# A graph layer on one core: ScalarE copies the last 16 items, and GpSimd makes every low part of h

## The chip, the core and the metric

The kernel runs on one core of a Trainium2 chip. The core has five engines that run their own instruction streams and meet at semaphores: TensorE (PE in the profile), VectorE (DVE), ScalarE (ACT), GpSimd (POOL), and SyncE (SP), which here only issues transfers. The metric is the device time of one execution in microseconds, lower is better.

## What is computed

```python
def _L0_gnn_ref(user_feat, item_feat, adj, W_item, b_item, W_user, b_user):
    h = item_feat @ W_item.T + b_item        # 10000 x 128
    b = user_feat @ W_user.T + b_user        # 10000 x 128
    return jax.nn.relu(adj @ h + b)          # adj is 10000 x 10000
x = _layernorm(x + _L0_gnn_ref(x, L0_gnn_item_feat, adj, ...), axis=-1)
```

Everything is float32. The product `adj @ h` is nearly all of the work: 400 MB of `adj` are read once and multiplied.

## The kernel before

**Products in parts.** TensorE takes operands of type fp32r, float32 rounded to fewer bits. So each operand is split: a high part (the rounded copy, made by ScalarE) and a low part (the value minus its high part, made by a subtraction). `adj @ h` is then three products: high x high and high x low (both read `adj_hi`; the second uses `h_lo`), and low x high (`adj_lo` with `h_hi`).

**Groups and tiles.** The users are cut into 20 groups, 19 of 512 and one of 272. Within a group TensorE adds up over 78 full chunks of 128 items, in 20 tiles of four chunks; a full tile is 12 matmuls of 128x512. The last tile (t = 19, `LAST`) has two full chunks, one chunk for `x @ W_user.T` (its weights are `h_hi` and `h_lo` at place `USER`), and one packed matmul, `h_pack` with `tail_pack`, for the last 16 items and the bias.

**Pipeline of `adj`.** SP loads a tile of 1 MB into one of five slots (`ADJ_RING`) once `lo_made` says that VectorE has finished with what was in it. ScalarE makes `adj_hi` (`split_hi`, L519), VectorE makes `adj_lo` (`split_lo`, L714, a `tensor_tensor` with two inputs in SBUF), both in four slots (`PART_RING`): the high part of a tile waits until TensorE is through with the tile four before it. TensorE waits for `hi_made`, does eight matmuls, waits for `lo_made`, does four.

**Start.** Before group 0, TensorE projects the items (`project_items`, L440) into four PSUM buffers, VectorE adds the bias (`add_item_bias`, L679) into `h_full`, ScalarE makes `h_hi` (`split_h`, L536), and GpSimd (t = 0 to 8, L640) or VectorE (t = 9 to 19, `split_h_lo`, L697) makes `h_lo`. The last projection (L444) reads `items_tail`, three copies of the last 16 items, which VectorE puts in place (`copy_items_tail`, L690). Tile 0 of `adj` is split in two halves between these steps (L526 on ScalarE, L722 on VectorE). After its last `h_lo`, GpSimd also makes one row group of `h_pack` (L645) and the low part of `w_user` (L649). In group 0 TensorE waits for `h_lo` of tile t before tile t, and before tile 19 also for `h_pack` and for `w_lo_made`, the signal of L649.

**Order of the work.** Each engine's order is that in which the code calls it; small tables of tile numbers (`HIGH_HALF_AFTER`, `LOW_HALF_AFTER`, `LATE_BLOCK_AFTER`, `POOL_LOWS`, `LOW_BLOCKS_FROM`) say after which tile a step stands. From group 1 on, the engines also do the layer norm of the group before; there GpSimd has two instructions in each group (L657 and L661).

Of the kernel before, what the change touches and what calls it, by code (L numbers as in the profile page):

```python
# [26 lines left out]
P = 128  # L27
# [46 lines left out]
LATE_BLOCK_AFTER = {3: 16, 5: 17, 7: 18, 9: 19}  # L74
TAIL_AFTER_ADD = 16
POOL_LOWS = 9
LOW_BLOCKS_FROM = 4

# [121 lines left out]
def gnn_kernel(nc, adj_t, adj_tail, x_t, adj_narrow, tail_narrow, x_narrow, item_t, w_item_bias, w_user_t, b_user, out, out_last):  # L200
    with ExitStack() as ctx:
# [74 lines left out]
        h_lo_made = sem("h_lo_made")  # L276
        h_lo_made_dve = sem("h_lo_made_dve")
        h_pack_made = sem("h_pack_made")
# [146 lines left out]
        def _(pe):  # L425
# [58 lines left out]
            for t in range(TILES):  # L484
                if t == LAST:
                    pe.wait_ge(w_lo_made, 1)
                    pe.wait_ge(h_pack_made, 1)
                if t < POOL_LOWS:
                    pe.wait_ge(h_lo_made, t + 1)
                else:  # L490
                    pe.wait_ge(h_lo_made_dve, t + 1 - POOL_LOWS)
                tile_product(0, t, 0)
# [10 lines left out]
        def _(act):  # L503
# [24 lines left out]
            def split_h(t):  # L528
# [6 lines left out]
                k = t * PER_TILE  # L535
                nc.scalar.copy(h_hi[:, k:k + n, :], h_full[:, k:k + n, :]).then_inc(h_hi_made, 1)  # L536

            def gather(n):
# [67 lines left out]
            for t in range(EARLY_BLOCKS):  # L606
                split_h(t)
                if t in HIGH_HALF_AFTER:
                    split_hi_half(HIGH_HALF_AFTER.index(t))
            for t in range(1, TILES):  # L610
                if t == LAST:
# [16 lines left out]
        def _(pool):  # L628
# [6 lines left out]
            nc.gpsimd.memset(items_tail[:, :], 0.0).then_inc(items_tail_zeroed, 1)  # L635
            for t in range(POOL_LOWS):
                n = full_chunks(t)
# [4 lines left out]
            again = slice(PACK_HI_AGAIN, PACK_HI_AGAIN + PACKED_ROWS)  # L642
            pool.wait_ge(h_lo_made, POOL_LOWS)
            pool.wait_ge(h_hi_made, TILES)
            nc.gpsimd.tensor_tensor(h_pack[again, :], h_tail[again, :],  # L645
# [26 lines left out]
        def _(dve):  # L672
            def add_item_bias(t):
# [3 lines left out]
                if t == LAST:  # L677
# [3 lines left out]
                                        ALU.add).then_inc(h_full_made, 1)  # L681

            def copy_items_tail():

                dve.wait_ge(items_tail_zeroed, 1)
                dve.wait_ge(item_landed[item_load(LAST)], 16)
                cols = (FULL - LAST * PER_TILE) * P
                landed = item_tiles(LAST, cols + TAIL)[:, cols:cols + TAIL]
                packs = items_tail[:, 0:len(PACKS) * PACK_LO].rearrange("p (n c) -> p n c", c=PACK_LO)[:, :, 0:TAIL]
                nc.vector.tensor_copy(packs, landed[:, None, :].to_broadcast([P, len(PACKS), TAIL])).then_inc(  # L690
                    items_tail_made, 1)

            def split_h_lo(t):
                n = full_chunks(t)
                k = t * PER_TILE
                dve.wait_ge(h_hi_made, t + 1)
                nc.vector.tensor_tensor(h_lo[:, k:k + n, :], h_full[:, k:k + n, :],  # L697
                                        h_hi[:, k:k + n, :].bitcast(F32), ALU.subtract).then_inc(h_lo_made_dve, 1)

# [130 lines left out]
            for t in range(TILES):  # L830
                add_item_bias(t)
                if t == TAIL_AFTER_ADD:
                    copy_items_tail()
                if t in LOW_HALF_AFTER:
                    split_lo_half(LOW_HALF_AFTER.index(t))
            for t in range(1, TILES):
                split_lo(0, t)
                if t >= LOW_BLOCKS_FROM and POOL_LOWS + t - LOW_BLOCKS_FROM < TILES:
                    split_h_lo(POOL_LOWS + t - LOW_BLOCKS_FROM)
            group(1, 1)  # L840
# [52 lines left out]
```

## Time and profile before

| | |
|---|---|
| three runs | 1086.23, 1086.39, 1086.84 us (median 1086.39) |
| the profiled execution | 1085.97 us, of which the span of the trace is 1084.1 us |
| TensorE busy | 1078.3 us, 99% of the span |
| VectorE, ScalarE, GpSimd busy | 962.1, 835.7 and 115.8 us |
| granted TensorE clock | 0.999 |
| transfers | 417.14 MB, 385 GB/s over the span |

In the timeline each row has the start from the beginning of the span, the time that it took, engine, line, operation, what is written and read with shapes, how many instructions are merged in the row, and, in brackets, how long the engine stood idle before it and what ended that. An engine starts its next instruction some 0.1 us before the recorded end of the one before when nothing holds it back, so a merged row is shorter than its instructions added up. A wait on a transfer is shown as DMA. PEld is the loading of weights into TensorE, which runs beside the matmuls.

### The profile page before, as it was taken

The page shows a single profiled execution, that of the slowest core. Times are in us where ns is not written, and L with a number is a line of the kernel's source. Part 1 is how long each engine was busy: PE and PEld are TensorE (multiplying, and loading weights), DVE is VectorE, ACT ScalarE, POOL GpSimd, SP SyncE. Part 2 cuts the span into 40 slices and gives each one's busy share as a digit, 9 for nine tenths or more (in the row PEclk, how much of TensorE's full clock was granted, in tenths as well). Part 3 has the DMA queues.
Part 4 walks back from the last instruction along what each step waited for, and adds up shares of the span by engine and source line. Part 5 has one row for each costly group of instructions (what it writes and reads, how often), then busy time and mean ns, then how long its engine had stood idle before and what let it go on. Part 6 is the DMA issues. An engine that isn't in the chain of part 4 may idle for free.

```text
span 1084.1 us, 14876 instructions
## 1 busy us (share of the span) xinstructions
PE 1078.3 (99%) x4935; PEld 901.3 (83%) x4935; DVE 962.1 (89%) x614; ACT 835.7 (77%) x801; POOL 115.8 (11%) x56
## 2 busy tenths in 40 slices
PE   9999999999999999999999999999999999999998
PEld 9888888888888888888888888888888888888888
DVE  6998898989898989898989898989898989898987
ACT  5877787878787878787878787878787878787775
POOL 4270000000000000000000000000000000000001
PEclk9999999999999999999999999999999999999999
DMA  9999999999999999999999999999999999999993
GB/s 356 419 382 420 352 422 356 422 370 423 366 422 360 422 376 423 364 422 355 423 359 422 362 423 358 423 359 422 364 422 358 421 358 422 359 422 359 419 350 154
DMA packets 66408, 417.14 MB, mean 385 GB/s; under 512 B 8194, under 2 KB 9284, under 8 KB 20052
## 3 DMA queue, kind: packets, MB, share of 16 engines
q1 hardware_dynamic: 66100, 416.68, 96.5%
q8 instruction: 13, 0.21, 0.1%
q10 hardware_dynamic: 288, 0.20, 0.1%
q14 instruction: 7, 0.06, 0.0%
HBM read 411.72 MB, written 5.12 MB: 385 GB/s over the span
## 4 chain that ended last, share of the span: by engine, by line
PE 99%; DVE 1%; DMA 0%; issue 0%; SPq 0%; DVEq 0%
PE acc L458 32%; PE acc L457 32%; PE acc L464 32%; PE h_ps L440 1%; PE acc L461 0%; DMA items<-item_t 0%; DVE adj_lo L722 0%; DVE h_full L679 0%; DVE stats L781 0%; PE h_ps L444 0%; SPq L335 0%; DVE items L804 0%; SPq L399 0%; DVE items L797 0%; PE z_ps L472 0%
## 5 line engine op out<-in xcount | busy, mean ns | idle before, releaser
L714 DVE TENSOR_TENSOR adj_lo<-adj,adj_hi 128x2048 fp32r<-128x2048 f32 (+2 forms) x391 | 864.8, 2230 | 106.2 <-ACT adj_hi L519 105.8
L519 ACT CAST adj_hi<-adj 128x2048 fp32r<-128x2048 f32 (+2 forms) x391 | 724.3, 1864 | 144.1 <-DMA adj<-adj_t 95.4
L457 PE MATMUL acc<-adj_hi,h_hi 128*128 128x512 f32 (+1 forms) x1580 | 604.3, 384 | 0.0
L458 PE MATMUL acc<-adj_hi,h_lo 128*128 128x512 f32 (+1 forms) x1580 | 604.3, 384 | 0.0
L464 PE MATMUL acc<-adj_lo,h_hi 128*128 128x512 f32 (+1 forms) x1580 | 417.2, 384 | 0.0
L458 PEld LDWEIGHTS acc<-adj_hi,h_lo 128*128 128x128 f32 x1580 | 296.7, 188 | 58.4
L457 PEld LDWEIGHTS acc<-adj_hi,h_hi 128*128 128x128 f32 x1580 | 296.6, 188 | 58.4
L464 PEld LDWEIGHTS acc<-adj_lo,h_hi 128*128 128x128 f32 x1580 | 292.6, 188 | 58.4
L657 POOL TENSOR_TENSOR items<-items,minus_mean 128x512 f32<-128x512 f32 x19 | 39.3, 2068 | 586.4 <-ACT minus_mean L552 586.4
L661 POOL TENSOR_TENSOR items<-items,rstd_all 128x512 f32<-128x512 f32 x19 | 37.6, 1981 | 339.9 <-ACT rstd_all L573 339.9
L544 ACT COPY gathered<-part 32x16 f32<-32x16 f32 x152 | 30.8, 203 | 22.1 <-DVE part L752 12.3
L565 ACT ACTIVATE std<-total,eps 32x16 f32<-32x16 f32 x19 | 5.8, 308 | 44.4 <-DVE total L769 44.4
L645 POOL TENSOR_TENSOR h_pack<-h_tail,h_pack 17x128 fp32r<-17x128 f32 x1 | 26.1, 26053 | 27.8 <-ACT h_hi L536 27.8
L573 ACT COPY rstd_all<-rstd 32x16 f32<-32x16 f32 x76 | 15.4, 203 | 14.4 <-DVE rstd L776 13.7
L552 ACT ACTIVATE minus_mean<-total 32x16 f32<-32x16 f32 x76 | 16.2, 214 | 6.4 <-DVE total L763 5.5
L679 DVE TENSOR_TENSOR h_full<-h_ps,w_bias 128x512 f32<-128x512 f32 (+1 forms) x20 | 13.3, 674 | 7.4 <-PE h_ps L440 7.4
L536 ACT CAST h_hi<-h_full 128x512 fp32r<-128x512 f32 (+1 forms) x20 | 12.0, 606 | 8.0 <-DVE h_full L679 8.0
L709 DVE TENSOR_TENSOR tail_pack<-tail_in,tail_pack 16x512 fp32r<-16x512 f32 (+1 forms) x20 | 13.5, 676 | 0.6
L711 DVE TENSOR_TENSOR adj_lo<-xg,adj_hi 128x512 fp32r<-128x512 f32 (+1 forms) x20 | 13.8, 688 | 0.3
L746 DVE STREAM_TRANSPOSE items<-items 128x512 f32<-128x512 f32 x19 | 13.4, 704 | 0.0
L730 DVE SCALAR_TENSOR_TENSOR items<-acc,xg 128x512 f32<-128x512 f32 x19 | 13.0, 684 | 0.0
L752 DVE TENSOR_REDUCE part<-items 128x16 f32<-128x512 f32 x19 | 12.8, 675 | 0.0
(51 smaller groups left out, 153.8 us busy)
## 6 DMA issues: line engine op xcount, KB each, us to landing
adj<-adj_t SPq DMA_DIRECT2D x360, 1024.0 KB, 7.7
adj<-adj_t SPq DMA_DIRECT2D x21, 512.0 KB, 5.3
adj<-adj_narrow SPq DMA_DIRECT2D x11, 952.0 KB, 7.5
xg<-x_t SPq DMA_DIRECT2D x19, 256.0 KB, 8.0
out<-items SPq DMA_DIRECT2D x19, 256.0 KB, 2.3
tail_in<-adj_tail SPq DMA_DIRECT2D x57, 32.0 KB, 4.6
adj<-item_t SPq DMA_DIRECT2D x2, 512.0 KB, 6.7
adj<-item_t SPq DMA_DIRECT2D x1, 1024.0 KB, 8.7
```

The lines of the kernel that those rows point to most:

```text
L457: nc.tensor.matmul(into, h_hi[:, k, :], high[:, c, :], start=(k == 0), stop=False)
L458: nc.tensor.matmul(into, h_lo[:, k, :], high[:, c, :], start=False, stop=False)
L464: mm = nc.tensor.matmul(into, h_hi[:, k, :], low[:, c, :], start=False, stop=(k == FULL - 1))
L519: nc.scalar.copy(into[:, places[0]:places[-1] + 1, :], source[:, places[0]:places[-1] + 1, :]).then_inc(hi_made, 1)
L544: ins = nc.scalar.copy(gathered[:, q, :], part[q * SQ:q * SQ + SQ, :])
L552: ins = nc.scalar.mul(minus_mean[q * SQ:q * SQ + SQ, :], total[:, :], -1.0 / HID)
L573: ins = nc.scalar.copy(rstd_all[q * SQ:q * SQ + SQ, :], rstd_32[:, :])
L645: nc.gpsimd.tensor_tensor(h_pack[again, :], h_tail[again, :], h_pack[again, :].bitcast(F32), ALU.subtract).then_inc(h_pack_made, 1)
L657: nc.gpsimd.tensor_tensor(centred, z_b, minus_mean[:, :, None].to_broadcast([P, BANDS, SQ]), ALU.add).then_inc(centred_made, 1)
L661: nc.gpsimd.tensor_tensor(z_b, centred, rstd_all[:, :, None].to_broadcast([P, BANDS, SQ]), ALU.mult).then_inc(out_ready, 1)
L711: nc.vector.tensor_tensor(into[:, AT_USER, :], xg[:, 0:u], high[:, AT_USER, :].bitcast(F32), ALU.subtract).then_inc(lo_made, 1)
L714: nc.vector.tensor_tensor(into[:, places[0]:places[-1] + 1, :], source[:, places[0]:places[-1] + 1, :], high[:, places[0]:places[-1] + 1, ...
```

## The change

The copy of the last 16 items goes from VectorE (behind the bias of t = 16) to ScalarE (behind the second half of tile 0's high part). The low parts of h of t = 9 to 19 go from VectorE (one behind each of the subtractions of tiles 4 to 14) to GpSimd, behind its first nine. GpSimd's instructions for `h_pack` and `w_user` stay behind all of its low parts.

```diff
-TAIL_AFTER_ADD = 16
-POOL_LOWS = 9
-LOW_BLOCKS_FROM = 4
...
-                if t < POOL_LOWS:
-                    pe.wait_ge(h_lo_made, t + 1)
-                else:
-                    pe.wait_ge(h_lo_made_dve, t + 1 - POOL_LOWS)
+                pe.wait_ge(h_lo_made, t + 1)
                 tile_product(0, t, 0)
...
+            def copy_items_tail():
+
+                act.wait_ge(items_tail_zeroed, 1)
+                act.wait_ge(item_landed[item_load(LAST)], 16)
+                cols = (FULL - LAST * PER_TILE) * P
+                landed = item_tiles(LAST, cols + TAIL)[:, cols:cols + TAIL]
+                packs = items_tail[:, 0:len(PACKS) * PACK_LO].rearrange("p (n c) -> p n c", c=PACK_LO)[:, :, 0:TAIL]
+                nc.scalar.copy(packs, landed[:, None, :].to_broadcast([P, len(PACKS), TAIL])).then_inc(
+                    items_tail_made, 1)
...
                 if t in HIGH_HALF_AFTER:
                     split_hi_half(HIGH_HALF_AFTER.index(t))
+                if t == HIGH_HALF_AFTER[-1]:
+                    copy_items_tail()
...
-            for t in range(POOL_LOWS):
+            for t in range(TILES):
                 n = full_chunks(t)
                 k = t * PER_TILE
                 pool.wait_ge(h_hi_made, t + 1)
                 nc.gpsimd.tensor_tensor(h_lo[:, k:k + n, :], h_full[:, k:k + n, :],
                                         h_hi[:, k:k + n, :].bitcast(F32), ALU.subtract).then_inc(h_lo_made, 1)
             again = slice(PACK_HI_AGAIN, PACK_HI_AGAIN + PACKED_ROWS)
-            pool.wait_ge(h_lo_made, POOL_LOWS)
-            pool.wait_ge(h_hi_made, TILES)
+            pool.wait_ge(h_lo_made, TILES)
...
             for t in range(TILES):
                 add_item_bias(t)
-                if t == TAIL_AFTER_ADD:
-                    copy_items_tail()
                 if t in LOW_HALF_AFTER:
                     split_lo_half(LOW_HALF_AFTER.index(t))
             for t in range(1, TILES):
                 split_lo(0, t)
-                if t >= LOW_BLOCKS_FROM and POOL_LOWS + t - LOW_BLOCKS_FROM < TILES:
-                    split_h_lo(POOL_LOWS + t - LOW_BLOCKS_FROM)
```

The removed functions `copy_items_tail` and `split_h_lo` of VectorE held the same operations with VectorE's own semaphore for `h_lo`.

VectorE's order around the end of the start and the first tiles of group 0, before the change (from the second half of tile 0 on; the pair of L697 and L714 then repeats up to tile 15):

```order
L722 TENSOR_TENSOR adj_lo<-adj,adj_hi 128x1024
L679 TENSOR_TENSOR h_full<-h_ps,w_bias 128x512
L690 COPY items_tail<-items 128x3x16
L679 TENSOR_TENSOR h_full<-h_ps,w_bias 128x512 x2
L678 TENSOR_TENSOR h_tail<-h_ps,w_bias 128x128
L679 TENSOR_TENSOR h_full<-h_ps,w_bias 128x256
L714 TENSOR_TENSOR adj_lo<-adj,adj_hi 128x2048 x4
L697 TENSOR_TENSOR h_lo<-h_full,h_hi 128x512
```

The same place in the changed kernel, up to tile 19 (there L709 is the half of tile 0, L683 the bias, L701 the low part of an `adj` tile, L696 and L698 the packed tail and the user chunk of tile 19):

```order
L709 TENSOR_TENSOR adj_lo<-adj,adj_hi 128x1024
L683 TENSOR_TENSOR h_full<-h_ps,w_bias 128x512 x3
L682 TENSOR_TENSOR h_tail<-h_ps,w_bias 128x128
L683 TENSOR_TENSOR h_full<-h_ps,w_bias 128x256
L701 TENSOR_TENSOR adj_lo<-adj,adj_hi 128x2048 x18
L696 TENSOR_TENSOR tail_pack<-tail_in,tail_pack 16x512
L698 TENSOR_TENSOR adj_lo<-xg,adj_hi 128x512
```

The copy and the eleven `h_lo` are gone, and the subtractions of tiles 1 to 18 stand one behind the other.

GpSimd's order before the change, from its last step of preparation to the first instruction of the layer norm:

```order
L635 MEMSET items_tail 128x128
L640 TENSOR_TENSOR h_lo<-h_full,h_hi 128x512 x9
L645 TENSOR_TENSOR h_pack<-h_tail,h_pack 17x128
L649 TENSOR_TENSOR h_lo<-w_user,h_hi 128x128
L657 TENSOR_TENSOR items<-items,minus_mean 128x512
```

And in the changed kernel:

```order
L640 MEMSET items_tail 128x128
L645 TENSOR_TENSOR h_lo<-h_full,h_hi 128x512 x19
L645 TENSOR_TENSOR h_lo<-h_full,h_hi 128x256
L649 TENSOR_TENSOR h_pack<-h_tail,h_pack 17x128
L653 TENSOR_TENSOR h_lo<-w_user,h_hi 128x128
L661 TENSOR_TENSOR items<-items,minus_mean 128x512
```

Eleven more low parts stand ahead of `h_pack` and of `w_user`'s low part.

## Rows read from the trace of the kernel before

**Rows 1.** The page: the chain that ended last, shares of the span by engine.

```profile
PE 99%; DVE 1%; DMA 0%; issue 0%; SPq 0%; DVEq 0%
```

**Rows 2.** Timeline, TensorE: last projections, tiles 0 and 1, start of tile 19.

```profile
18.16 5.08 PE L440 MATMUL h_ps<-w_bias,items 128*128 128x128 f32 x44
23.37 0.30 PEld L444 LDWEIGHTS h_ps<-w_bias,items_tail 128*128 128x128 f32 x2 [0.33 <-DVE items_tail L690]
...
23.62 0.47 PE L457 MATMUL acc<-adj_hi,h_hi 128*128 128x512 f32 x1
...
26.46 0.39 PE L457 MATMUL acc<-adj_hi,h_hi 128*128 128x512 f32 x1
...
28.28 1.07 PE L464 MATMUL acc<-adj_lo,h_hi 128*128 128x512 f32 x4
...
75.42 0.39 PE L457 MATMUL acc<-adj_hi,h_hi 128*128 128x512 f32 x1
```

**Rows 3.** Timeline, VectorE, 19 to 82 us.

```profile
19.06 1.22 DVE L722 TENSOR_TENSOR adj_lo<-adj,adj_hi 128x1024 fp32r<-128x1024 f32 x1
...
23.14 0.18 DVE L690 COPY items_tail<-items 128x48 f32<-128x48 f32 x1
...
25.48 2.29 DVE L714 TENSOR_TENSOR adj_lo<-adj,adj_hi 128x2048 fp32r<-128x2048 f32 x1 [0.45 <-ACT adj_hi L519]
...
35.22 0.68 DVE L697 TENSOR_TENSOR h_lo<-h_full,h_hi 128x512 fp32r<-128x512 f32 x1
...
63.59 8.89 DVE L714 TENSOR_TENSOR adj_lo<-adj,adj_hi 128x2048 fp32r<-128x2048 f32 x4
72.51 0.83 DVE L709 TENSOR_TENSOR tail_pack<-tail_in,tail_pack 16x512 fp32r<-16x512 f32 x1
73.36 0.86 DVE L711 TENSOR_TENSOR adj_lo<-xg,adj_hi 128x512 fp32r<-128x512 f32 x1
74.14 7.92 DVE L714 TENSOR_TENSOR adj_lo<-adj,adj_hi 128x1024 fp32r<-128x1024 f32 x4
```

**Rows 4.** Timeline, ScalarE, 19 to 71 us.

```profile
19.98 1.04 ACT L526 CAST adj_hi<-adj 128x1024 fp32r<-128x1024 f32 x1
...
23.54 1.92 ACT L519 CAST adj_hi<-adj 128x2048 fp32r<-128x2048 f32 x1 [1.40 <-DMA adj<-adj_t]
26.03 1.92 ACT L519 CAST adj_hi<-adj 128x2048 fp32r<-128x2048 f32 x1 [0.58 <-DMA adj<-adj_t]
...
62.19 1.92 ACT L519 CAST adj_hi<-adj 128x2048 fp32r<-128x2048 f32 x1 [0.54 <-DMA adj<-adj_t]
...
69.90 0.29 ACT L613 CAST h_hi<-w_user 128x128 fp32r<-128x128 f32 x1
```

**Rows 5.** Timeline, GpSimd, 7 to 74 us.

```profile
7.36 1.27 POOL L640 TENSOR_TENSOR h_lo<-h_full,h_hi 128x512 fp32r<-128x512 f32 x1 [5.72 <-ACT h_hi L536]
9.06 9.92 POOL L640 TENSOR_TENSOR h_lo<-h_full,h_hi 128x512 fp32r<-128x512 f32 x8 [0.43 <-ACT h_hi L536]
46.75 26.05 POOL L645 TENSOR_TENSOR h_pack<-h_tail,h_pack 17x128 fp32r<-17x128 f32 x1 [27.77 <-ACT h_hi L536]
72.88 0.79 POOL L649 TENSOR_TENSOR h_lo<-w_user,h_hi 128x128 fp32r<-128x128 f32 x1
```

**Rows 6.** Timeline, VectorE and GpSimd in a later group.

```profile
209.41 2.29 DVE L714 TENSOR_TENSOR adj_lo<-adj,adj_hi 128x2048 fp32r<-128x2048 f32 x1 [0.19 <-ACT adj_hi L519]
...
210.30 2.31 POOL L657 TENSOR_TENSOR items<-items,minus_mean 128x512 f32<-128x512 f32 x1 [31.11 <-ACT minus_mean L552]
...
212.14 2.62 DVE L714 TENSOR_TENSOR adj_lo<-adj,adj_hi 128x2048 fp32r<-128x2048 f32 x1 [0.44 <-ACT adj_hi L519]
```

**Rows 7.** Timeline, GpSimd near the end, VectorE idle.

```profile
1075.82 1.05 POOL L661 TENSOR_TENSOR items<-items,rstd_all 128x512 f32<-128x512 f32 x1 [9.30 <-ACT rstd_all L573]
```

**Rows 8.** VectorE's groups of instructions by form, usual duration of L709 and L711 (us busy, mean ns).

```profile
L711 DVE TENSOR_TENSOR adj_lo<-xg,adj_hi 128x512 fp32r<-128x512 f32 x19 | 13.3, 701 | 0.3
L709 DVE TENSOR_TENSOR tail_pack<-tail_in,tail_pack 16x512 fp32r<-16x512 f32 x19 | 13.1, 689 | 0.6
```

More of the change, by code:

```diff
@@ L276, in gnn_kernel @@
         h_lo_made = sem("h_lo_made")
-        h_lo_made_dve = sem("h_lo_made_dve")
         h_pack_made = sem("h_pack_made")
@@ L681, in add_item_bias @@
                                         ALU.add).then_inc(h_full_made, 1)
[L683 to L698, printed above, removed]
             def split_lo(g, t):
```

## The prediction

> **What bounds the kernel now.** I read the chain that ended last first: 99% of it is TensorE, and transfers and issue are nothing [rows 1]. Then the timeline of TensorE: from the first product of tile 0 at 23.62 it does not stop; tile 1 begins at 26.46 and tile 19 at 75.42, 18 tiles in 48.96 us, 2.72 each, which is twelve matmuls of 0.227 with no gap [rows 2]. So the kernel is some 24 us of start and then a full TensorE. An edit can gain only in the start, and it costs whatever makes TensorE stand still even once, as nothing later makes that good. The change touches no matmul. What it touches are three things that TensorE waits for: `items_tail_made` before the last projection, `h_lo` of each tile, and the signal of L649 (low part of `w_user`) before tile 19.
>
> In the start, TensorE's last projection waited 0.33 us for VectorE's copy [rows 2, 3]. In group 0, VectorE is ahead of need by little: the low part of tile 1 ended at 25.48 + 2.29 = 27.77 and was read at 28.28 [rows 2, 3]. GpSimd's last two signals come at 46.75 + 26.05 = 72.80 and 72.88 + 0.79 = 73.67, the second 1.75 us before tile 19 [rows 2, 5]. That 1.75 us is the cover that this prediction is about.
>
> **How the two engines share.** The strangest row is GpSimd's L645: 17x128 elements, 26.05 us. It was released at 46.75 and ended at 72.80, and in that whole time VectorE went from one two-input subtraction into the next without a gap; the first place where one ended before the next began is 63.59 + 8.89 = 72.48 to 72.51, and 0.32 us later L645 was done [rows 3, 5]. So a waiting GpSimd instruction doesn't get its turn between two VectorE instructions that follow closely; it needs an opening, and 0.03 us is one. The next one agrees: L649 was released at 72.88 and ended 0.33 us after the opening at 73.34 [rows 3, 5].
>
> VectorE pays for it. L709 took 0.83 in place of 0.69 and L711 0.86 in place of 0.70 [rows 3, 8]: 0.15 us each for a GpSimd instruction 128 wide, with the opening 0.18. For 512 wide there is a later group: VectorE's L714 ended at 211.70, GpSimd's L657 at 212.61, 0.91 later, and the next L714, issued at 212.14, took 2.62 in place of 2.29; so it was held until 211.70 + 0.77 [rows 6]. Alone, this kind of instruction takes 1.05, so 0.14 lie before the hold [rows 7]. But `h_lo` isn't that kind: it writes fp32r, and takes 1.27, or 1.24 in a row [rows 5]. With the same 0.14 before and 0.14 behind, it holds VectorE 1.27 - 0.28 = 0.99 us. The low bound is the 0.77 of L657. I take 0.98, because the 0.33 of L649, which is also fp32r, fits a line through 1.13 at 512 (2.1 ns per column and nearly no fixed part).
>
> The Trainium skill, "SBUF — State Buffer", section "Who interferes with whom", says that a VectorE instruction with two SBUF inputs and a GpSimd instruction that reads SBUF exclude each other, the later one waiting until the first finishes. The exclusion agrees with L645 and L709; "until the first finishes" does not, as L645 sat through more than ten of them. By the page the sum below would be that of the second rival.
>
> **The change part by part.** (1) The copy on ScalarE. It stands behind L526, which ends at 21.02 [rows 4]. Its load is the one that tiles 18 and 19 of the items came from, and TensorE ran through these without a gap up to 23.24 (44 matmul halves in 5.08) [rows 2], so it had landed by some 22. ScalarE's next real deadline is the high part of tile 1, whose transfer lets it start only at 23.54 [rows 4]. So 0.2 us there cost nothing, and TensorE's last projection no longer waits: 23.37 becomes about 23.25, -0.1 us. Were the cover gone, the copy would cost its 0.2.
>
> (2) VectorE loses eleven L697 of 0.68, 0.60 each in a row [rows 3], 6.6 us. It wasn't what TensorE waited for, so this gains nothing; but it makes openings: L714 takes 2.20 in a row (8.89 for four, the last 2.29) [rows 3], and the high parts come 2.49 apart [rows 4]. That is 0.29 us per tile.
>
> (3) GpSimd's nine low parts end at 9.06 + 9.92 = 18.98, and the tenth is ready to go then, against VectorE's first half of tile 0, issued at 19.06 [rows 3, 5]. Whoever is first, each half is late by at most one hold. The bias steps between them read only one SBUF input and GpSimd's eight in a row kept 1.24 beside them [rows 5], so GpSimd uses these: about four passes, t = 9 to 12, by 26. TensorE needs the half tiles only in tile 0, some 4 us later, and tile 1's low part at 28.2; it now ends at 27.8 to 28.9. SP loads tile 5 behind the second half and tile 6 behind tile 1's low part; ScalarE was a tile ahead of TensorE all along, which covers a microsecond there. Cost 0 to 0.7; I take 0.1, which cancels (1).
>
> (4) Then seven passes are left (t = 13 to 19; the last is 256 wide, hold 0.46), and each needs an opening. A pass makes VectorE late by 0.98, and at 0.29 per tile it has caught up, and the next opening is there, after three tiles. Counted in one: for the low part of t = 19 to go in ahead of tile 18, VectorE must have had room for the six before it. The high part of tile 1 ends at 25.46; that of tile 16 begins at 62.19 [rows 4], two more at 2.49 put the end of tile 18's at 69.1. Less 17 subtractions at 2.20 (37.4), the room is 69.1 - 25.5 - 37.4 = 6.2 us. Needed: 6 x 0.98 = 5.9, and some 0.5 of the pass that still runs when tile 1 is due, 6.4. So by 0.2 us it isn't there. Then the last low part goes into the opening ahead of L709 (about 71.5, needed at 75.4), `h_pack` into the one ahead of L711 (72.6), and both of the openings that served L645 and L649 before are taken. With a hold of 0.77 the need is 4.6 + 0.5 = 5.1, and it all fits; the point from which it decides is (6.2 - 0.5) / 6 = 0.95 us.
>
> (5) L649 is late next. Behind L711 come the 1024-wide part of tile 19 and three L714 of group 1, and before the change these ran in one row from 74.14 to 82.06 [rows 3]. TensorE stands at 75.4 before all of tile 19, as it waits there first. The high part of group 1's fourth tile needs tile 19 done, so VectorE runs dry after the third L714 at the latest, and that opening can't be missed. VectorE is about a microsecond earlier than before, as it has no L697: 81.2, plus 0.33, is 81.5. Stall 81.5 - 75.4 = 6.1 us. If it catches up one L714 earlier, 79.0, the stall is 3.9; by the row before as it stands, 7.0. I take 5.9 as I hold the latest opening to be the likelier. Once TensorE goes on, its buffers are full, and nothing is added.
>
> Sum: -0.1 + 0.1 + 5.9, against the profiled execution's own 1085.97 (span 1084.10 and 1.87 around it), 1091.9; that execution is 0.4 below the median of 1086.39. I say **1092.0**.
>
> **The rivals.** *It all fits* (not slower; 0.39). GpSimd's hold is nearer 0.77, or one more pass goes by before tile 1; the margin is 0.2 us in 6.4, so this is nearly as likely. L649 then waits only for its input (69.9 before [rows 4]) and takes the opening ahead of L709, 1.7 us or more before need. Time: 1086.4, up to 1087.1 with what (3) may cost.
>
> *Turn by turn* (0.04). If a waiting GpSimd instruction comes in after each VectorE one, the seven passes follow each other from tile 1 on, at 2.20 + 0.98 = 3.18 per tile against TensorE's 2.72: 7 x 0.46 = 3.2, less 0.5 of slack, 2.7 lost: 1089.1. L645 speaks against it.
>
> *GpSimd keeps the way* (0.08). Its instructions in a row (1.24 apart) may leave no opening for VectorE either. At 19.0 five low parts are ready; VectorE's first half waits for 5 x 1.24 less the 0.1, up to 6, and with it the bias that the last projections wait for; less 0.9 us of slack there, TensorE starts 5.2 later: 1091.6. In favour is only symmetry; against it, between two such rows GpSimd's hold lapses for 1.24 - 0.98 = 0.26 us.
>
> *Worse than forecast* (0.04). With a hold over 1.0, or openings that have to be longer, low parts of t = 18 or 19 come late themselves, each for one more wait: 1093.5 to 1096.
>
> **How the numbers follow.** The forecast has 0.43, in its own range 1089.8 to 1093.1 (stalls of 3.4 to 7.0). That leaves 0.02 for a gain over 0.2%, 2.2 us, about what a measurement of this kernel can tell from none: nothing in the start can give it, since the copy is worth 0.1. Slower over 0.2%: forecast, turn by turn, GpSimd first, worse, together 0.59. The same 0.39. The range has to hold both the not slower case and the forecast: 1086.1 to 1093.2 leaves out some 0.1.
>
> **What would show it.** In the profile after: on TensorE one idle stretch of 4 to 7 us at about 75.4, ahead of tile 19, ended by GpSimd's L653, and none before; GpSimd's L645 rows of 2 to 8 us from 27 us on, each ending 1.1 us after a VectorE instruction; VectorE rows of 2.9 to 3.2 where a pass went ahead. A row of `w_user`'s low part that ends by 75 makes the prediction wrong, and then the holds show why: VectorE rows stretched by 0.77 less the gap, not by 0.98. An idle TensorE at 21 to 24 us would be the last but one rival.

## The result and the profile after

The changed kernel took 1089.88 us (median of six runs, 1089.73 to 1092.33), the kernel before 1086.31 (six runs on the same chip, 1086.05 to 1087.07): a ratio of 1.0033, 95% interval 1.0022 to 1.0044, slower by 3.6 us. The profiled execution took 1089.83 us, with a span of 1087.8 us and a granted clock of 1.000, so it is 3.86 us above the profiled execution before. Of all executions reported below, four took 1198 us and more, one of them of the kernel before; they count in the medians and not in the ratios.

In the chain that ended last, against [rows 1], TensorE's share went from 99% to 96%, VectorE's from 1% to 3%, and that of transfers from 0% to 1%:

```profile
PE 96%; DVE 3%; DMA 1%; SPq 0%; issue 0%; DVEq 0%
```

The timeline of TensorE answers to [rows 2]. Tile 0 begins at 23.72 in place of 23.62 and tile 1 at 26.54 in place of 26.46. But the low x high part of tile 1 now waits, and so does that of each of the five tiles behind it:

```profile
23.72 0.48 PE L453 MATMUL acc<-adj_hi,h_hi 128*128 128x512 f32 x1
...
28.91 1.20 PE L460 MATMUL acc<-adj_lo,h_hi 128*128 128x512 f32 x4 [0.39 <-DVE adj_lo L701]
29.94 0.39 PE L453 MATMUL acc<-adj_hi,h_hi 128*128 128x512 f32 x1
...
79.09 0.39 PE L453 MATMUL acc<-adj_hi,h_hi 128*128 128x512 f32 x1
```

The first products of tiles 2 to 7 begin at 29.94, 33.25, 36.56, 39.84, 43.15 and 46.45, 3.28 to 3.31 apart; from tile 7 on every tile takes 2.72 again, and tile 19 begins at 79.09. Before, tile 2 began at 29.18 and tile 19 at 75.42. So 3.67 us of the loss are there at tile 19: 0.76 at the start of tile 2, and 2.91 in the five tiles 2 to 6. Nothing is lost ahead of tile 19, where the prediction had put it.

The waits in 24 to 50 us, in total, times and longest, name the same line, once for the weights and once for the matmul:

```profile
PEld acc L460 <- DVE adj_lo L701: 4.3, 6, 0.8
PE acc L460 <- DVE adj_lo L701: 1.8, 6, 0.4
```

VectorE's timeline answers to [rows 3]. There a subtraction of 128x2048 took 2.29. Now five in succession, those of tiles 2 to 6, take 3.37 to 3.38, and the first one behind them 2.28 again (the rows are read one by one, so each has its own duration):

```profile
19.47 1.35 DVE L709 TENSOR_TENSOR adj_lo<-adj,adj_hi 128x1024 fp32r<-128x1024 f32 x1
...
21.95 2.33 DVE L709 TENSOR_TENSOR adj_lo<-adj,adj_hi 128x1024 fp32r<-128x1024 f32 x1
...
26.53 2.32 DVE L701 TENSOR_TENSOR adj_lo<-adj,adj_hi 128x2048 fp32r<-128x2048 f32 x1
28.78 3.38 DVE L701 TENSOR_TENSOR adj_lo<-adj,adj_hi 128x2048 fp32r<-128x2048 f32 x1
32.08 3.37 DVE L701 TENSOR_TENSOR adj_lo<-adj,adj_hi 128x2048 fp32r<-128x2048 f32 x1
...
41.98 3.38 DVE L701 TENSOR_TENSOR adj_lo<-adj,adj_hi 128x2048 fp32r<-128x2048 f32 x1
45.28 2.28 DVE L701 TENSOR_TENSOR adj_lo<-adj,adj_hi 128x2048 fp32r<-128x2048 f32 x1
47.48 2.83 DVE L701 TENSOR_TENSOR adj_lo<-adj,adj_hi 128x2048 fp32r<-128x2048 f32 x1
50.23 2.54 DVE L701 TENSOR_TENSOR adj_lo<-adj,adj_hi 128x2048 fp32r<-128x2048 f32 x1
...
74.77 0.83 DVE L696 TENSOR_TENSOR tail_pack<-tail_in,tail_pack 16x512 fp32r<-16x512 f32 x1
```

GpSimd's timeline shows the other side, and answers to [rows 5]:

```profile
26.66 3.35 POOL L645 TENSOR_TENSOR h_lo<-h_full,h_hi 128x512 fp32r<-128x512 f32 x1
29.96 3.34 POOL L645 TENSOR_TENSOR h_lo<-h_full,h_hi 128x512 fp32r<-128x512 f32 x1
33.27 3.34 POOL L645 TENSOR_TENSOR h_lo<-h_full,h_hi 128x512 fp32r<-128x512 f32 x1
...
40.86 2.35 POOL L645 TENSOR_TENSOR h_lo<-h_full,h_hi 128x512 fp32r<-128x512 f32 x1 [0.96 <-ACT h_hi L529]
46.83 1.34 POOL L645 TENSOR_TENSOR h_lo<-h_full,h_hi 128x256 fp32r<-128x256 f32 x1 [3.62 <-ACT h_hi L529]
48.24 2.39 POOL L649 TENSOR_TENSOR h_pack<-h_tail,h_pack 17x128 fp32r<-17x128 f32 x1
72.76 2.30 POOL L653 TENSOR_TENSOR h_lo<-w_user,h_hi 128x128 fp32r<-128x128 f32 x1 [22.13 <-ACT h_hi L618]
```

Read the two together. Low part t = 14 is issued at 26.66, while VectorE subtracts for tile 1. That subtraction ends at 26.53 + 2.32 = 28.85; the low part ends at 26.66 + 3.35 = 30.01, 1.16 later, and VectorE's next, issued at 28.78, takes 1.10 longer than the 2.28 of an undisturbed one. At 29.96 low part 15 waits in the same way. Every VectorE instruction is followed by one GpSimd instruction, although VectorE leaves no gap. A VectorE turn and a GpSimd turn together take 32.08 - 28.78 = 3.30 us, against TensorE's 2.72. The 256-wide pass costs 2.83 - 2.28 = 0.55, and `h_pack` 0.26; VectorE then has room for these. L653 ended at 75.06, 4.03 before tile 19 began. It says nothing on turns, as it came in ahead of L696, where VectorE had a gap of 0.03 (74.74 to 74.77).

The Trainium skill, "SBUF — State Buffer", says in its section "Who interferes with whom" that two such instructions contend for a shared pair of ports, and in its "Summary: rules for kernel authors" that the second one to issue is blocked until the first finishes. Rows 28.78 to 50.23 agree with it; the 26.05 us of L645 in [rows 5] do not.

### The profile page after: what moved, and what is told of

Read it like the earlier page. It is cut to its first block, busy times and chain, and to the rows that moved or that the text cites. A ratio compares the mean times of both kernels' runs of the same rounds, so it can differ in the third digit from the quotient of the medians.

```text
span 1087.8 us, 14875 instructions
## 1 busy us (share of the span) xinstructions
PE 1079.9 (99%) x4935; PEld 900.6 (83%) x4935; DVE 964.0 (89%) x602; ACT 837.0 (77%) x802; POOL 118.8 (11%) x67
## 4 chain that ended last, share of the span: by engine, by line
PE 96%; DVE 3%; DMA 1%; SPq 0%; issue 0%; DVEq 0%
PE acc L460 32%; PE acc L454 32%; PE acc L453 32%; DVE adj_lo L701 2%; PE h_ps L436 1%; DMA items<-item_t 1%; PE acc L457 0%; DVE h_full L683 0%; DVE adj_lo L709 0%; SPq L331 0%; DVE stats L768 0%; DVE items L791 0%; SPq L395 0%; DVE items L784 0%; PE z_ps L468 0%
## 5 line engine op out<-in xcount | busy, mean ns | idle before, releaser
L701 DVE TENSOR_TENSOR adj_lo<-adj,adj_hi 128x2048 fp32r<-128x2048 f32 (+2 forms) x391 | 871.3, 2246 | 106.7 <-ACT adj_hi L512 105.3
L645 POOL TENSOR_TENSOR h_lo<-h_full,h_hi 128x512 fp32r<-128x512 f32 (+1 forms) x20 | 36.2, 1850 | 10.3 <-ACT h_hi L529 10.3
L576 ACT COPY rstd_all<-rstd 32x16 f32<-32x16 f32 x76 | 15.4, 203 | 14.4 <-DVE rstd L763 13.7
L683 DVE TENSOR_TENSOR h_full<-h_ps,w_bias 128x512 f32<-128x512 f32 (+1 forms) x20 | 13.2, 673 | 7.9 <-PE h_ps L436 7.9
L696 DVE TENSOR_TENSOR tail_pack<-tail_in,tail_pack 16x512 fp32r<-16x512 f32 (+1 forms) x20 | 13.5, 676 | 0.6
L698 DVE TENSOR_TENSOR adj_lo<-xg,adj_hi 128x512 fp32r<-128x512 f32 (+1 forms) x20 | 13.6, 680 | 0.3
```

What stands on the lines that cost most here:

```text
L576: ins = nc.scalar.copy(rstd_all[q * SQ:q * SQ + SQ, :], rstd_32[:, :])
L645: nc.gpsimd.tensor_tensor(h_lo[:, k:k + n, :], h_full[:, k:k + n, :], h_hi[:, k:k + n, :].bitcast(F32), ALU.subtract).then_inc(h_lo_made, 1)
L698: nc.vector.tensor_tensor(into[:, AT_USER, :], xg[:, 0:u], high[:, AT_USER, :].bitcast(F32), ALU.subtract).then_inc(lo_made, 1)
L701: nc.vector.tensor_tensor(into[:, places[0]:places[-1] + 1, :], source[:, places[0]:places[-1] + 1, :], high[:, places[0]:places[-1] + 1, ...
```

## The experiments

Three sets were run, each beside its own runs of the kernel before, with medians of 1086.25 (26 runs), 1086.19 (33) and 1086.32 (21). A tile's time is the distance from its first product on TensorE to that of the next tile. "Profiled" is the one execution with a trace, from which the rows and the tiles' times come; where kernels spread widely its own time is named.

**Half the width.** The same work on GpSimd, with the low parts of t = 14 to 19 in two instructions each. Against the changed kernel:

```diff
-                nc.gpsimd.tensor_tensor(h_lo[:, k:k + n, :], h_full[:, k:k + n, :],
-                                        h_hi[:, k:k + n, :].bitcast(F32), ALU.subtract).then_inc(h_lo_made, 1)
+                cuts = (0, n) if t < 14 else (0, n // 2, n)
+                for p, q in zip(cuts, cuts[1:]):
+                    low = nc.gpsimd.tensor_tensor(h_lo[:, k + p:k + q, :], h_full[:, k + p:k + q, :],
+                                                  h_hi[:, k + p:k + q, :].bitcast(F32), ALU.subtract)
+                low.then_inc(h_lo_made, 1)
```

> The changed kernel with GpSimd's low parts of t = 14 to 19 each made by two instructions of half the width. Turns (GpSimd gets in once after each VectorE subtraction and holds it 1.10 us per 512 columns): each L701 is stretched by 0.55, 2.75 us per tile against TensorE's 2.72, so only the start and tile 1 cost anything, 1087.1 us (1086.7 to 1087.5), tiles 2 to 6 at 2.72 to 2.78. Work (the cost is the sum of what GpSimd has left to do, however it is cut): the hold adds up to the same, 1089.9. Opening (what the prediction assumed): 1086.4 or 1090 and more, with TensorE idle ahead of tile 19.

Measured: 1087.46 (ten runs, two of them 1092.83 and 1092.57), ratio 1.0020 (1.0006 to 1.0034); profiled 1087.06. VectorE and GpSimd, one row of each:

```profile
28.83 2.82 DVE L704 TENSOR_TENSOR adj_lo<-adj,adj_hi 128x2048 fp32r<-128x2048 f32 x1
29.47 2.79 POOL L647 TENSOR_TENSOR h_lo<-h_full,h_hi 128x256 fp32r<-128x256 f32 x1
```

The same turns, but each holds VectorE for 0.54, so a pair of turns takes 2.75 in place of 3.30, and tiles 2 to 12 take 2.72 to 2.77. Tile 2 begins at 30.00, as in the changed kernel (29.94). So what tiles 2 to 6 lost hangs on the width of one turn: with the same columns in narrower turns, tiles 2 to 12 lose 0.3 in all, in place of 2.9.

**One at a time.** Full width, but low parts t = 14 to 19 are released by VectorE's steps for tiles 4, 6, 8, 10, 12 and 14:

```diff
                 pool.wait_ge(h_hi_made, t + 1)
+                if t >= 14:
+                    pool.wait_ge(lo_made, steps_to(0, 4 + 2 * (t - 14)))
```

> The changed kernel with the low parts of t = 14 to 19 on GpSimd released one by one, after the low parts of adj tiles 4, 6, 8, 10, 12 and 14. Turns: one stretch of 1.10 us in two tiles, 5.50 against TensorE's 5.44, is hidden; left is the start and tile 1, 1087.0 us (1086.6 to 1087.4). Work: 1089.9, since GpSimd does all of the same and in the same stage.

Measured: 1086.93 (ten runs), ratio 1.0007 (0.9997 to 1.0017).

```profile
35.70 3.20 POOL L647 TENSOR_TENSOR h_lo<-h_full,h_hi 128x512 fp32r<-128x512 f32 x1 [8.91 <-DVE adj_lo L703]
...
37.67 3.38 DVE L703 TENSOR_TENSOR adj_lo<-adj,adj_hi 128x2048 fp32r<-128x2048 f32 x1
```

Each pass still stretches one subtraction to 3.38. But one hold of 1.10 every two tiles meets 2 x (2.72 - 2.20) = 1.04 of room and what VectorE was ahead: tile 2 takes 2.75 and every one from 3 on 2.72. Tile 2 begins at 30.05 and tile 19 at 76.32, which is 0.87 and 0.90 later than before: nearly all that is left came before tile 2. With the run above, this shows it for tiles 2 to 6: the same passes cost 0.03 there if they do not follow each other.

**Fourteen on GpSimd.** The kernel before with `POOL_LOWS = 14` in place of 9: VectorE makes the rest from tile 4 on. It was to measure the start alone.

> The kernel before with GpSimd making the low parts of t = 0 to 13 in place of 0 to 8, VectorE t = 14 to 19 behind adj tiles 4 to 9; the copy stays on VectorE. By both theories only what GpSimd does in the start is left: tile 1 late by some 0.7 us, 1087.1 us (1086.7 to 1087.5). If that share of the loss is nothing, 1086.4. It also has L645 wait among VectorE's subtractions with no other GpSimd work: by turns it takes 2 to 3 us, as in the changed kernel; if it needs an opening, until about 72 us, as in the kernel before.

Measured: 1089.78 (ten runs, 1087.16 to 1092.90), ratio 1.0026 (1.0017 to 1.0036). The expected 1087.1 is wrong. The profiled execution is the slowest, 1092.90, and shows something new, on VectorE and GpSimd:

```profile
19.18 6.07 DVE L722 TENSOR_TENSOR adj_lo<-adj,adj_hi 128x1024 fp32r<-128x1024 f32 x1
19.23 1.27 POOL L640 TENSOR_TENSOR h_lo<-h_full,h_hi 128x512 fp32r<-128x512 f32 x1
20.46 1.27 POOL L640 TENSOR_TENSOR h_lo<-h_full,h_hi 128x512 fp32r<-128x512 f32 x1
...
22.91 1.26 POOL L640 TENSOR_TENSOR h_lo<-h_full,h_hi 128x512 fp32r<-128x512 f32 x1
...
49.55 10.53 POOL L645 TENSOR_TENSOR h_pack<-h_tail,h_pack 17x128 fp32r<-17x128 f32 x1 [25.38 <-ACT h_hi L536]
```

GpSimd did four passes while VectorE's half tile of 1.22 us stood at 19.18 and got in only when GpSimd had nothing left, at 24.2. TensorE began tile 0 at 28.98. This is the prediction's rival in which GpSimd keeps the way, 5.4 us late where 5.2 were worked out. That the two agree is partly luck, for the sum left out TensorE's clock:

```profile
26.00 2.90 PE L440 MATMUL h_ps<-w_bias,items 128*128 128x128 f32 x12 [4.10 <-DVE h_full L679]
```

TensorE stood for 4.10 us, and from 26.00 to 31.68 its granted clock was 0.50, 1.2 GHz in place of 2.4. Tile 0 took 4.20 in place of 2.84, and tile 19 began at 82.15, 6.73 late. The other nine executions have no trace, so what a usual one of 1089.8 loses isn't shown. GpSimd's `h_pack` took neither the 2 to 3 us nor the wait until about 72 that were expected: it was passed over until a gap of VectorE at 59.8.

The rival did not come in the changed kernel's profiled execution: there the half tile of 19.47 took 1.35.

**The copy back on VectorE**, all low parts still on GpSimd. Against the changed kernel (the function itself moves with it):

```diff
-                if t == HIGH_HALF_AFTER[-1]:
-                    copy_items_tail()
...
                 add_item_bias(t)
+                if t == 16:
+                    copy_items_tail()
```

> The changed kernel with the copy of the last 16 items back on VectorE. Turns: 1089.9 us to 1090.2. Rival, that the moved copy is what costs: 1086.4.

Measured: 1090.34 (five runs, 1089.29 to 1092.21), ratio 1.0045 (1.0031 to 1.0059); profiled 1089.29.

```profile
24.64 0.66 DVE L682 COPY items_tail<-items 128x48 f32<-128x48 f32 x1
```

The loss is that of the low parts. The copy, 0.18 in [rows 3], is held by GpSimd too. It stands behind the held halves of tile 0, and TensorE waited 1.75 us for it and began tile 0 at 25.60, where the changed kernel began at 23.72. So beside the moved low parts the copy on ScalarE does bring the start forward; in these two profiles that gained nothing by tile 19 (78.55 and 79.09), presumably since a TensorE that starts later asks later for VectorE's low parts.

**The copy alone on ScalarE.** The kernel before, with the copy taken from VectorE:

```diff
+                if t == HIGH_HALF_AFTER[-1]:
+                    copy_items_tail()
...
                 add_item_bias(t)
-                if t == TAIL_AFTER_ADD:
-                    copy_items_tail()
```

> The kernel before with only the copy of the last 16 items moved to ScalarE; the low parts stay as before. Its last projection no longer waits for VectorE's copy (0.33 us), and in the three profiles with the moved copy tile 0 began 0.1 to 0.4 us earlier than in the kernel before; the low part of tile 1 (27.77 before) is needed at 27.9 to 28.2 then, so nothing takes it back: 1085.9 us (1085.7 to 1086.2). Rival, that the share is nothing: 1086.25.

Measured: 1086.14 (11 runs), ratio 0.9999 (0.9990 to 1.0008). The copy's move is worth nothing that the times can show: 1085.9 was expected and 1086.25 for no effect, and 1086.14 doesn't tell them apart. In the profile tile 0 begins at 22.89, 0.73 earlier than before, and tile 19 at 75.09, 0.33 earlier. (The expectation misreads one profile: in the changed kernel tile 0 began 0.10 later than before, not earlier.)

**The start paced as well.** Low parts 9 and 10 wait for VectorE's two halves of tile 0, t = 12 to 17 for tiles 4, 6, ... 14, and 18 and 19 for tile 15. Against the changed kernel:

```diff
+                if t in (9, 10):
+                    pool.wait_ge(lo_made, t - 8)
+                if t >= 12:
+                    pool.wait_ge(lo_made, steps_to(0, 4 + 2 * (t - 12)) if t < 18 else steps_to(0, 15))
```

> The changed kernel with every low part of t = 9 on released so that GpSimd is never two instructions in a row beside a VectorE subtraction of two SBUF inputs: t = 9 and 10 after the halves of tile 0, t = 12 to 17 after adj tiles 4, 6, 8, 10, 12, 14, t = 18 and 19 after 15. Turns, with the price in the sequence and not in the amount: 1085.9 to 1086.7 us, tile 1 at most 0.3 late, and no execution above 1087.5, since GpSimd never has a row of ready instructions with which to keep VectorE out. Work: 1089.9.

Measured: 1087.00 (median of 11), ratio 1.0005 (0.9995 to 1.0015); profiled 1086.73. The median lies above the 1085.9 to 1086.7 expected. Tile 2 begins at 28.96, 1.1 earlier than with only the later passes paced, so the 0.8 to 0.9 at the start of tile 2 were those of the passes t = 9 to 13. But now GpSimd has three low parts and `h_pack` in a row at the end, and tiles 17 and 18 take 3.14 and 2.90 (tile 5, behind the pass released by tile 4, takes 2.92):

```profile
63.36 9.28 POOL L649 TENSOR_TENSOR h_lo<-h_full,h_hi 128x512 fp32r<-128x512 f32 x3 [2.29 <-DVE adj_lo L705]
72.71 2.38 POOL L653 TENSOR_TENSOR h_pack<-h_tail,h_pack 17x128 fp32r<-17x128 f32 x1
```

**Why did `h_pack` wait 26 us?** Turns explain the change, but not the row from which the prediction had its rule. Four kernels, all made from the kernel before, ask for that. First, `h_pack` asked for later, at the start of a subtraction:

```diff
             pool.wait_ge(h_hi_made, TILES)
+            pool.wait_ge(lo_made, steps_to(0, 15))
```

> The kernel before with GpSimd's L645 released by the low part of adj tile 15 (about 65.8 us) and not by the last high part of h (46.6). Time as before, 1086.25 us. Missed turn (a request that comes in the last 0.5 us of the other engine's instruction isn't served at its end, and then not until an opening): L645 now asks at the start of a 2.2 us subtraction and takes 2.4 us, ending at 68.4. Rival, that this row of subtractions lets nothing in: it ends at 72.8 as before.

Measured: 1086.15 (median of ten), ratio 1.0001 (0.9991 to 1.0011).

```profile
65.99 6.75 POOL L646 TENSOR_TENSOR h_pack<-h_tail,h_pack 17x128 fp32r<-17x128 f32 x1 [47.24 <-DVE adj_lo L715]
```

VectorE's next instructions were issued at 67.94 and 70.14, in a row, and then, after a gap of 0.03, at 72.45; only that gap was of use to GpSimd. So it isn't the moment within an instruction at which GpSimd asks. The other traces agree: the requests that were passed over came 0.03 to 1.8 us after the start of a VectorE instruction, those that were served 0.1 to 2.2.

Second, five small subtractions on GpSimd ahead of it, released by the high parts of tiles 4 to 8 (a buffer no longer needed takes them):

```diff
+            pool.wait_ge(tile_done, 1)
+            for t in range(4, 9):
+                pool.wait_ge(hi_made, steps_to(0, t))
+                nc.gpsimd.tensor_tensor(items_tail[:, :], h_hi[:, t, :].bitcast(F32), h_hi[:, t + 1, :].bitcast(F32),
+                                        ALU.subtract).then_inc(probed, 1)
+                pool.wait_ge(probed, t - 3)
```

> The kernel before with five extra GpSimd subtractions (128x128, into items_tail, which nothing reads any more) released by the high parts of adj tiles 4 to 8, ahead of L645; they add work and change no output. Turns alone: each waits at most for one VectorE instruction and holds the next by 0.25 us; 1086.3 to 1086.9 us. Missed turn: the one for tile 4 asks early in a 2.2 us subtraction and ends within 2.6 us; the one for tile 5 asks in the last 0.3 us of the short L697, and it and all that stand behind it, L645 and L649 too, wait for openings: TensorE stands for 5 us and more ahead of tile 19, 1091 us and more.

Measured: 1087.74 (ten runs, 1087.16 to 1088.80), ratio 1.0014 (1.0004 to 1.0023); above the one expectation and below the other.

```profile
46.86 0.83 POOL L653 TENSOR_TENSOR h_pack<-h_tail,h_pack 17x128 fp32r<-17x128 f32 x1 [2.24 <-ACT h_hi L537]
70.61 3.32 POOL L657 TENSOR_TENSOR h_lo<-w_user,h_hi 128x128 fp32r<-128x128 f32 x1 [22.92 <-ACT h_hi L614]
```

Now `h_pack`, the same instruction at the same place, is served at once, and it is L657, 22.9 us after GpSimd's last instruction, that is passed over until VectorE's gap at 73.6. VectorE made its own low parts here at 2.80 per tile and had no room for the holds: tiles 9 to 14 take 2.79 to 2.99.

Third, one execution with probes further apart, and two more behind `h_pack` (`probe(hi, lo, n)` is a subtraction as above, released by the high part of tile `hi` or the low part of tile `lo`):

```diff
+            pool.wait_ge(tile_done, 1)
+            probe(4, 0, 1)
+            probe(8, 0, 2)
             pool.wait_ge(h_hi_made, TILES)
...
             pool.wait_ge(h_pack_made, 1)
+            probe(0, 10, 3)
+            probe(0, 13, 4)
             pool.wait_ge(w_hi_made, 1)
```

> The kernel before with extra GpSimd subtractions of 128x128 that change no output: two ahead of L645, released by the high parts of tiles 4 and 8, and two between L645 and L649, released by the low parts of tiles 10 and 13. What is open is why the same GpSimd instruction is sometimes served at the end of the next VectorE instruction and sometimes only at an opening. Long pause (it is shut out when the two engines haven't met for some 20 us): all of these are served within 3 us, as the pauses are 4 to 12 us, and L649 too. Rival, that L645 is served or not by its instant alone: one of the two behind it sits until about 72 us, and TensorE stands before tile 19.

Measured: 1087.32. Every one is served, also `w_user`'s:

```profile
43.19 1.00 POOL L646 TENSOR_TENSOR items_tail<-h_hi 128x128 f32<-128x128 f32 x1 [7.68 <-ACT adj_hi L520]
46.19 1.08 POOL L655 TENSOR_TENSOR h_pack<-h_tail,h_pack 17x128 fp32r<-17x128 f32 x1 [2.00 <-ACT h_hi L537]
...
70.17 1.67 POOL L661 TENSOR_TENSOR h_lo<-w_user,h_hi 128x128 fp32r<-128x128 f32 x1 [7.75 <-ACT h_hi L614]
```

Fourth, one execution with six memsets on GpSimd right ahead of `h_pack`, in case GpSimd's own idleness was the cause:

```diff
+            pool.wait_ge(tile_done, 1)
+            for n in range(6):
+                nc.gpsimd.memset(items_tail[:, :], 0.0).then_inc(probed, 1)
+                pool.wait_ge(probed, n + 1)
```

> The kernel before with six GpSimd memsets (which read nothing) right ahead of L645; they write items_tail, which nothing reads any more. If L645 is shut out because GpSimd itself had stood idle for 28 us, it is served now, within 3 us. If it is the long unbroken run of VectorE, in which the two haven't met on their inputs, it is shut out as before, until about 72.5 us. The time is that of before either way, 1086.2 us.

Measured: 1086.07.

```profile
46.48 1.52 POOL L648 MEMSET items_tail<- 128x128 f32 x6 [27.60 <-ACT h_hi L537]
48.08 24.95 POOL L650 TENSOR_TENSOR h_pack<-h_tail,h_pack 17x128 fp32r<-17x128 f32 x1
```

The memsets aren't held (six in 1.52 us, beside a VectorE whose rows keep 2.29 and 0.69), and `h_pack` waits as before. So being at work does not help; the two probe kernels suggest that what helps is to have met VectorE lately.

**Two attempts at a faster kernel.** In the first, fourteen low parts on GpSimd with t = 9 and t = 11 held until VectorE's two halves are done. Against "fourteen on GpSimd":

```diff
+                if t in (9, 11):
+                    pool.wait_ge(lo_made, (t - 7) // 2)
```

> The kernel fourteen with two waits added: GpSimd starts on t = 9 only after the first half of tile 0 has its low part, and on t = 11 only after the second. If the loss and the spread of fourteen (1087.2 to 1092.9 us) come from GpSimd's instructions in a row keeping VectorE out at about 19 us, both go: 1086.3 to 1087.0 us, no execution above 1087.6, and the half tile takes at most 2.3 us. If they come from the amount that GpSimd does in the start, nothing changes: about 1089.8.

Measured: 1087.14 (ten runs, three of them 1089.3 to 1090.8), ratio 1.0012 (1.0003 to 1.0021). The two waits take 2.6 us from the median of 1089.78, which supports that VectorE's half behind GpSimd's row is what costs there. But they don't cure it wholly, and the kernel isn't faster than before. The profiled execution is the slowest, 1090.84, and shows what is left:

```profile
26.57 0.68 PE L444 MATMUL h_ps<-w_bias,items_tail 128*128 128x128 f32 x2 [2.19 <-DVE items_tail L692]
```

The second half of tile 0 began late, at 22.85 behind ScalarE's, and took 2.20, and the copy behind it was held to 0.94. TensorE stood 2.19 us for the copy, and its granted clock from 26.90 to 29.61 was 0.50; tile 0 began 3.28 late and took 4.34 in place of 2.84.

In the second, the copy is on ScalarE, VectorE makes t = 9 to 14 behind tiles 4 to 9, and GpSimd t = 15 to 19, released by tiles 8, 10, 12, 14 and 15. Against the kernel before (the copy's move is left out):

```diff
-            for t in range(POOL_LOWS):
+            for t in (*range(POOL_LOWS), *range(15, TILES)):
...
+                if t >= 15:
+                    pool.wait_ge(lo_made, steps_to(0, {15: 8, 16: 10, 17: 12, 18: 14, 19: 15}[t]))
...
-                if t >= LOW_BLOCKS_FROM and POOL_LOWS + t - LOW_BLOCKS_FROM < TILES:
+                if t >= LOW_BLOCKS_FROM and POOL_LOWS + t - LOW_BLOCKS_FROM < 15:
```

> A version from the findings: the copy on ScalarE; VectorE makes the low parts of t = 9 to 14 behind adj tiles 4 to 9, GpSimd those of 15 to 19, one at a time, released by the low parts of tiles 8, 10, 12, 14 and 15. In tail_only, tiles 13 to 17 lost 0.2 us since VectorE had no slack left; here it has five instructions less. Turns: 1085.9 us (1085.6 to 1086.3), no tile from 3 on above 2.75 us. If GpSimd's lone passes are shut out as L645 was, TensorE waits for a low part at tile 15: 1089 and more.

Measured: 1087.03 (11 runs), ratio 1.0004 (0.9995 to 1.0013); profiled 1088.28. Expected was a small gain.

```profile
46.63 6.61 POOL L655 TENSOR_TENSOR h_lo<-h_full,h_hi 128x512 fp32r<-128x512 f32 x1 [28.42 <-DVE adj_lo L719]
...
53.20 3.35 POOL L655 TENSOR_TENSOR h_lo<-h_full,h_hi 128x512 fp32r<-128x512 f32 x1
55.32 3.38 DVE L719 TENSOR_TENSOR adj_lo<-adj,adj_hi 128x2048 fp32r<-128x2048 f32 x1
```

The first of these low parts was passed over until 52.08, where VectorE issued its next subtraction as the last one ended and not some 0.08 earlier; the second had come due meanwhile, and two holds in a row made tiles 11 and 12 take 2.99 and 3.31. No kernel beat the one before.

## Why the prediction was right and where it was wrong

The direction was right and the time lies in the range, but not for the reason that the forecast gave, and that is luck: the range was drawn wide enough for the forecast and for no loss, and the loss that came by another way, 3.6 us where 5.6 were forecast, fell between them. What came is the rival "Turn by turn", which had a chance of 0.04.

- **Step (1), the copy.** Right: 0.23 us at 21.32 on ScalarE, and no gain or loss that can be measured when it is done alone.
- **Step (2), VectorE's eleven low parts gone.** Right that it gains nothing: TensorE was full before. (The eleventh is 256 wide and took 0.41, so it is 6.3 us and not 6.6.)
- **Step (3), the start.** The place was right, the size was not: 0.1 was taken and 0 to 0.7 given, and it cost 0.76 by the start of tile 2, of which 0.10 was there at tile 0. The halves of tile 0 became 1.35 and 2.33 in place of 1.22, and VectorE began tile 1's low part at 26.53 in place of 25.48 [rows 3]. "TensorE needs the half tiles only in tile 0" left out that bias steps and tile 1's low part queue behind them on VectorE, with only some 0.5 us in hand.
- **Step (4) is the one that failed**: "each needs an opening". It was made from L645's 26.05 us. In the changed kernel GpSimd had its turn behind every subtraction from the start of group 0, without openings. The count of the room, 6.2 against 6.4, hence had no bearing.
- **The hold** was put at 0.98 and is 1.10, so a pair of turns takes 3.30, not 3.18.
- **Step (5), `w_user` late**, falls with step (4): all low parts and `h_pack` were done by 50.63, and L653 found the opening ahead of L696 free, and was done 4 us early.
- **Turn by turn** was priced at 7 x 0.46 - 0.5 = 2.7. Measured: 5 x 0.58 = 2.9 in tiles 2 to 6, and the 0.76 before, 3.67. Its seven passes were five full ones, as t = 13 still went in beside the bias steps; the 256-wide pass and `h_pack` were absorbed. So this sum came near in part by errors that cancel: too many passes, each put too low.

The row that had been held against it was true, but of another situation, and the probes point to which. When L645 asked at 46.75 [rows 5], VectorE had gone on for 13.7 us without a gap, and had met no GpSimd instruction for longer; its last gap before had been this, in the trace of the kernel before:

```profile
33.01 2.29 DVE L714 TENSOR_TENSOR adj_lo<-adj,adj_hi 128x2048 fp32r<-128x2048 f32 x1 [0.25 <-ACT adj_hi L519]
```

In the changed kernel the two had been meeting since 19 us.

What the prediction said would show the theory wrong was there at once: `w_user`'s low part done by 75.06, just past the 75 named, no idle TensorE at tile 19, and VectorE rows of 3.38 where it had named 2.9 to 3.2. The reason that it named for such a case, a hold nearer 0.77, was wrong too: the rows were stretched by 1.10.

## What to carry to other kernels

Before a step is moved to an engine that shares a path with another, work out the pace of both in turns (here 2.20 + 1.10 against the 2.72 of TensorE), and release such steps singly, no faster than the slack per tile pays for them; the same passes cost 2.9 us in a row and 0.03 when spaced. A single very long row is evidence of one situation, not a rule: look at what both engines had done before it. And an engine whose work is off the chain gains nothing by being relieved.

## What was not expected of the hardware

**Who asks late may be passed over.** Two-input subtractions on VectorE and GpSimd took turns at the end of each instruction in all runs where they met often. In other cases the one that asked was left waiting until a gap, 0.03 us being enough. For GpSimd these cases bear on it, in us before it asked:

| GpSimd asks | VectorE's run without a meeting or a gap | since the last meeting | |
|---|---|---|---|
| first probe, in both probe kernels | 0.1 | 14.6, 14.7 | served |
| other probes and `w_user` in the third kernel | up to 7.9 | up to 7.9 | served |
| `h_lo` in "one at a time" | 8.9 | 8.9 | served |
| `h_pack` in "the copy alone" | 13.5 | 27.6 | shut out, 26.35 |
| `h_pack` before; first `h_lo` in the last kernel | 13.7 | 27.8, 28.4 | shut out, 26.05 and 6.61 |
| `h_pack` behind memsets | 14.9 | 29.2 | shut out, 24.95 |
| `h_pack` in "fourteen" with two waits | 19.0 | 19.0 | shut out, 15.45 |
| `w_user` behind the five probes | 22.9 | 22.9 | shut out, 3.32 |
| `h_pack` asked for later | 24.6 | 47.2 | shut out, 6.75 |
| `h_pack` in "fourteen" | 25.4 | 25.4 | shut out, 10.53 |

So the change of behaviour lies between 8.9 and 13.5 us of an unbroken run of VectorE, if a gap counts as much as a meeting. That isn't shown: the time since the last meeting alone sorts these cases as well, with the change between 14.7 and 19.0. What in the chip makes it so, and whether it is a time or a count, is open.

On the other side, VectorE asked for the first half of tile 0 while GpSimd worked through its low parts. It was served behind a row of 10.2 us ("half the width"), 10.3 ("one at a time") and 12.1 (the changed kernel, and "the copy back on VectorE"), and shut out for four passes in "fourteen", behind 12.35, or 11.1 if one counts from 8.10, where GpSimd's second pass came 0.03 later than in a close row. Length alone thus doesn't explain this one case. It also differs in its instant: VectorE asked 0.08 before the end of GpSimd's pass, and 0.25 to 0.92 before it in the four that were served. One execution can't tell.

The slowest executions of three kernels with these passes in a row would fit the same: one of the changed kernel at 1092.33, two of ten at half the width (1092.57 and 1092.83), two of five with the copy back (1092.18 and 1092.21). But none of them has a trace, and "one at a time", with the same start, had none in ten above 1087.42.

**Prices.** A GpSimd subtraction of 128x512 with fp32r output holds VectorE 1.10 us, 256 wide 0.55, 128 wide 0.26; VectorE's copy of 128x48 was held for 0.48 (0.66 against 0.18), and GpSimd's memsets neither hold nor are held.
